# Image strips of eight rows in place of eight columns, and the last image stored in three parts

## The chip, the cores and the metric

The kernel runs on one core of one Trainium2 chip, with its five engines: PE (matmuls), DVE, ACT, POOL, and SP, which here only issues transfers. The metric is the device time of one execution in microseconds, the median of several runs.

## The reference, cut to what matters

The input is 32 images of 128 channels and 56 x 56 pixels in fp32; the output has the same shape. Each image passes through two residual blocks:

```python
x = x + _L0_conv_ref(_gn(x), ...)   # a gate for each channel, from the channel means
x = x + _L1_conv_ref(_gn(x), ...)   # dilated local attention

# in _L1_conv_ref, with KS = 3 and DILS = (1, 2, 4):
value = _conv1x1(x, v_w, v_b)
keyf  = _proj(x, k1_w, ..., k2_be, k2_m, k2_v)    # conv1x1, bn, relu, twice
query = _proj(x, q1_w, ..., q2_be, q2_m, q2_v)
uk = jnp.concatenate([_unfold3(keyf, d) for d in DILS], axis=2)    # 27 neighbours
uv = jnp.concatenate([_unfold3(value, d) for d in DILS], axis=2)
sim = jax.nn.softmax(jnp.sum(uk * query[:, :, None], axis=1, keepdims=True), axis=2)
return _conv1x1(jnp.sum(sim * uv, axis=2), w_w, w_b)
```

The 27 neighbours lie at steps of 1, 2 and 4 pixels, in rows and columns alike, so that the neighbourhood stays the same when rows and columns of the image change places. Group norm takes means over whole channels, in which the order of the pixels does not matter.

## The kernel before, in words

Channels lie on the 128 partitions. An image is one contiguous run of 3136 fp32 numbers in each partition of the tile `raw`, which has four such buffers (`RAWS`). The kernel cuts each image into seven strips of eight image columns (56 x 8 pixels, `SPIX` = 448), and each strip into seven units of 8 x 8 pixels. Attention runs over 25 tiles of two units. A tile takes a score matmul (`scores`, L473), a mask with a running minimum on DVE (`masked`, L1036), an exponential on ACT (L652), a scaling on DVE (`scaled`, L1050 and L1053), two transposes (L487), a copy on ACT (L667) and the matmuls with the values into `ps_o` (`context`, L508 and L513).

Five operations of a strip read or write `raw` in the order of a strip:

- `hidden` (L527) is the first projection on PE. It streams the whole strip as the moving operand; PE takes an fp32 matmul in two passes, so that one `hidden` stands in the trace as two matmuls. The second projection (L534) streams the contiguous tile `hid` of the same size.
- `shifted` (L870) on POOL scales and shifts the strip in place, once PE has read it.
- `spread` (L897) on POOL copies normalised blocks, offset by four columns against the strips, into `xb`, with three instructions for a block (six for the first, which is made of two half blocks). These are the stationary operands of the value matmuls (`values`, L553).
- `final` (L1061) on DVE adds the attention's result from PSUM to the strip in place. It counts up `o_done`.

The channel sums (L1092) read the image in flat pieces of 448 numbers, and loads and stores move it whole.

The order of work is written out by hand. All engines walk through the same sequence of images and slots, 25 slots for an image, and tables such as `G_SLOT`, `X1_SLOT`, `V_SLOT` and `BLOCK_SLOT` give the slot at which a strip's step is issued, relative to slot 0 of its image (a negative number is a slot of the image before). Beside it runs a chain of small steps for the statistics of the images to come, at the slots in `CH`: p1, p3, p4, p7 and p11 are POOL's steps, d1 to d13 DVE's, c1 to c6 PE's, a4 and a6 ACT's. The waits of POOL in L811 (p1), L830 (p4) and L843 (p7) belong to it, as does DVE's L1136 (d9), a copy out of the PSUM bank `ps_v`, which `values` writes next.

On SP, `keys` and `values` issue copies between partitions, `load` fetches an image three ahead, and `store` writes an image once all seven strips are final. The store of an image is issued at slot `STORE` = 13 of the next one; the last image's at slot `FINAL` = 6 of the drain, the slots after the last image.

In the two accessors of `raw` the strip is a pattern of 56 steps of 56 numbers with 8 adjacent numbers each:

```python
raw[:, m.offset % RAWS, :].rearrange("p (r c) -> p r c", c=W)[:, :, SIDE * s:SIDE * (s + 1)]
```

Of the kernel before, what the change touches and what calls it, by code (L numbers as in the profile page):

```python
# [13 lines left out]
NIMG = 32  # L14
ROUND = 4
ROUNDS = (NIMG - 4) // ROUND
H = W = 56
# [9 lines left out]
STRIPS = 7  # L27
SIDE = 8
UPIX = SIDE * SIDE
SPIX = UNITS * UPIX  # L30
# [10 lines left out]
RAWS = 4  # L41
# [4 lines left out]
SCALE, TRANSPOSE, CONTEXT, FINAL = 1, 3, 5, 6  # L46
# [19 lines left out]
LOAD = 19  # L66
STORE = 13
PIECES = 4

AWAKE = {CH["c3"]: 9, CH["c4"]: 5}  # L70

# [126 lines left out]
def build(nc, x, par, w1, w2, wv, wo, bo, bv, wg, out):  # L198
    with ExitStack() as ctx:
# [46 lines left out]
        raw = sb("raw", [P, RAWS, RAWPIX])  # L246
# [37 lines left out]
        def strip_of(m, s):  # L284

            return raw[:, m.offset % RAWS, :].rearrange(
                "p (r c) -> p r c", c=W)[:, :, SIDE * s:SIDE * (s + 1)]

        in_par, in_w = sem("in_par"), sem("in_w")
        g_const = sem("g_const")  # L290
# [2 lines left out]
        in_wg = sem("in_wg")  # L293
        x_piece = [sem(f"x_piece{i}") for i in range(PIECES - 1)]
        g_zs = sem("g_zs")
# [37 lines left out]
        o_done = event("o_done", STRIPS)  # L333
# [40 lines left out]
        def col(c, n=1):  # L374
            return g1[:, c:c + n]
# [5 lines left out]
        def images(first, last, drain=0, register=None):  # L381

            with nc.Block() as block:
                @block.sync
                def _(sp):
# [3 lines left out]
                    def load(m):  # L389
                        sp.wait_ge(stored[m.parity()].sem, stored[m.parity()].count(m + -4, 16))  # L390
                        sp.wait_ge(x_in[m.parity()].sem, x_in[m.parity()].count(m + -2, 16))
                        if m.offset == 0:
                            for i in range(PIECES):
                                pixels = slice(2 * BATCH * i, min(2 * BATCH * (i + 1), RAWPIX))
                                sp.dma_start(raw[:, 0, pixels], x[m.index(), :, pixels]).then_inc(
                                    x_piece[i] if i < PIECES - 1 else x_in[0].next(16), 16)
                            return
# [2 lines left out]
                        sp.dma_start(raw[:, m.offset % RAWS, :],  # L400
                                     x[m.index(), :, :]).then_inc(x_in[m.parity()].next(16), 16)

                    def store(m):
                        sp.wait_ge(o_done.sem, o_done.count(m, STRIPS))
                        sp.dma_start(out[m.index(), :, :],
                                     raw[:, m.offset % RAWS, :]
                                     ).then_inc(stored[m.parity()].next(16), 16)

                    def keys(m, g):
# [27 lines left out]
                    def slot(n, t):  # L437
                        if t == (LOAD if n.offset != -1 else 0) and (n + 3).exists():
                            load(n + 3)
                        for m, rel in items_at(n, t):  # L440
                            for g, at in enumerate(g_slots(m)):
                                if rel == at + 2:
                                    keys(m, g)
                            for s in (1, 3, 5):
                                if rel == V_SLOT[min(s + 2, COLUMNS - 1)] + 1:
                                    values(m, s)
                        if t == (STORE if n.exists() else FINAL) and (n + -1).exists():
                            store(n + -1)

                    for n, t in slots(first, last, drain, register):  # L450
                        slot(n, t)
# [287 lines left out]
                def _(gp):  # L739
                    n = [0]  # L740
# [132 lines left out]
                    def spread(m, b):  # L873
                        i, half = divmod(b, 2)
                        if b == 0:
                            gp.wait_ge(pg.sem, pg.count(m, 31))
                            gp.wait_ge(x_in[m.parity()].sem, x_in[m.parity()].count(m, 16))
                            if m.offset == 0:
                                for piece in x_piece:
                                    gp.wait_ge(piece, 16)  # L880
                        gp.wait_ge(v_ps.sem, v_ps.count(m + -1, min(2 * i + 2, COLUMNS)))
                        rows = raw[:, m.offset % RAWS, :].rearrange("p (r c) -> p r c", c=W)
                        if b == COLUMNS - 1:
                            to = xb[:, i, :, :, :].rearrange("p n h k -> p (n h) k")[:, 0:CHUNKS, :]
                        else:
                            to = xb[:, i, :, half, :]
                        to = to.rearrange("p n (r c) -> p n r c", c=SIDE)
                        if b == 0:
                            parts = ((slice(0, HALO), slice(W - HALO, W)), (slice(HALO, SIDE), slice(0, HALO)))
                        else:  # L890
                            parts = ((slice(0, SIDE), slice(SIDE * b - HALO, SIDE * b + HALO)),)
                        for cs, at in parts:
                            for k, rs, src in ((0, slice(0, HALO), rows[:, H - HALO:H, at]),
                                               (0, slice(HALO, SIDE), rows[:, 0:HALO, at]),
                                               (slice(1, CHUNKS), slice(0, SIDE), rows[:, HALO:H - HALO, at].rearrange(
                                                   "p (n r) c -> p n r c", r=SIDE))):
                                last = gp.tensor_scalar(to[:, k, rs, cs], src, col(Y_A + m.parity()),  # L897
                                                        col(Y_B + m.parity()), ALU.mult, ALU.add)
                        last.then_inc(xb_done.next(), 1)
# [309 lines left out]
```

## Time and profile before

| what | us |
|---|---|
| median of 3 runs | 1479.59 (1479.5 to 1479.63) |
| the profiled execution's own time | 1480.63 |
| its span, from the first to the last instruction | 1478.9 |
| PE busy | 1445.5 |
| DVE busy | 1256.4 |
| ACT busy | 1169.7 |
| POOL busy | 914.7 |

All times below come from the profiled execution. It took 1.04 us more than the median of the runs, and 1.73 us of its time lie outside its span. The mean granted clock of PE was 0.997 of full speed.

### The profile page before, as it was taken

What the parts mean: (1) busy time and instruction counts of PE and PEld (TensorE: products, weight loads), DVE (VectorE), ACT (ScalarE), POOL (GpSimd) and SP (SyncE); (2) the same over time, 40 slices, a digit from 0 to 9 for tenths busy, and PEclk for the clock granted to TensorE, in tenths of its full rate; (3) what the DMA queues carried; (4) which work ended last, traced back from release to release, by engine and by line L of the source; (5) the groups of instructions that cost most, each with busy time, mean ns of one, the idle gap of its engine ahead of it and who ended that gap; (6) DMA issues with size and microseconds to landing.
All of it is one profiled execution on the core that took longest, in us unless ns stands there. A gap on an engine that the chain in (4) does not pass through costs nothing.

```text
span 1478.9 us, 34970 instructions
## 1 busy us (share of the span) xinstructions
PE 1445.5 (98%) x9123; PEld 1180.4 (80%) x9123; DVE 1256.4 (85%) x4602; ACT 1169.7 (79%) x3047; POOL 914.7 (62%) x2049
## 2 busy tenths in 40 slices
PE   5899999999999999999999999999999999999998
PEld 2688888888888888888888888888888888888886
DVE  7788888888888888888888888888888888888876
ACT  3688888788878788778788778888878888787886
POOL 5766566576666575665675665665665765665730
PEclk9999999999999999999999999999999999999999
DMA  3334554445554345554345554445544455544344
GB/s 137 86 95 151 171 154 127 119 144 154 161 163 127 110 144 163 155 166 117 113 148 167 155 156 109 128 151 170 155 127 122 140 154 164 161 127 112 101 117 145
DMA packets 104706, 205.95 MB, mean 139 GB/s; under 512 B 13632, under 2 KB 83776, under 8 KB 96448
## 3 DMA queue, kind: packets, MB, share of 16 engines
q1 hardware_dynamic: 103632, 203.49, 46.4%
q8 instruction: 79, 1.29, 0.4%
q14 instruction: 115, 0.94, 0.2%
q10 hardware_dynamic: 880, 0.23, 0.1%
HBM read 51.62 MB, written 51.38 MB: 70 GB/s over the span
## 4 chain that ended last, share of the span: by engine, by line
PE 96%; issue 1%; POOL 1%; ACT 0%; DVE 0%; ACTq 0%; POOLq 0%; DVEq 0%
PE ps_s L473 24%; PE ps_o L508 20%; PE ps_v L553 12%; PE ps_t L487 12%; PE ps_p L527 11%; PE ps_p L534 11%; PE ps_o L513 3%; PE ps_v L573 0%; PE ps_v L576 0%; PE ps_v L569 0%; PE ps_v L580 0%; PE ps_t L534 0%; ACT qq L686 0%; POOL hats L831 0%; ACT hid L675 0%
## 5 line engine op out<-in xcount | busy, mean ns | idle before, releaser
L652 ACT ACTIVATE e<-e,zmin 128x256 f32<-128x256 f32 x800 | 403.1, 504 | 154.4 <-DVE zmin L1036 150.6
L1036 DVE CUSTOM_DVE_ANT_0 e<-ps_s,mask 128x256 f32<-128x256 f32 x800 | 337.3, 422 | 146.8 <-PE ps_s L473 138.6
L508 PEld LDWEIGHTS ps_o<-eT,v 128*128 128x128 f32 x2688 | 380.3, 191 | 82.9 <-issue 70.2
L508 PE MATMUL ps_o<-eT,v 128*128 128x128 f32 x2688 | 430.3, 275 | 0.4 <-ACT eT L667 0.3
L473 PE MATMUL ps_s<-kk,qq 128*128 128x256 f32 x1408 | 427.6, 386 | 1.7 <-DVE zmin L1036 1.7
L897 POOL TENSOR_SCALAR xb<-raw,g 128x32 f32<-128x32 f32 (+3 forms) x768 | 353.8, 476 | 0.0
L487 PE MATMUL ps_t<-ident,e 128*128 128x128 f32 x1600 | 305.7, 273 | 0.0
L487 PEld LDWEIGHTS ps_t<-ident,e 128*128 128x128 f32 x1600 | 225.2, 141 | 80.5 <-issue 0.2
L667 ACT ACTIVATE eT<-ps_t 128x512 f32<-128x512 f32 (+1 forms) x416 | 236.8, 569 | 63.9 <-PE ps_t L487 60.5
L1053 DVE SCALAR_TENSOR_TENSOR e<-e,rz,keep 128x256 f32<-128x256 f32 x480 | 254.6, 530 | 17.1
L473 PEld LDWEIGHTS ps_s<-kk,qq 128*128 128x128 f32 x1408 | 223.6, 192 | 49.0 <-issue 40.5
L553 PE MATMUL ps_v<-wvoT,xb 128*128 128x128 f32 x1580 | 214.7, 276 | 3.8 <-issue 0.2
L527 PE MATMUL ps_p<-raw,w1x 128*128 128x448 f32 x448 | 207.7, 545 | 1.1 <-ACT hid L675 0.7
L534 PE MATMUL ps_p<-hid,w2T 128*128 128x448 f32 x442 | 203.9, 543 | 1.8 <-ACT hid L675 1.8
L553 PEld LDWEIGHTS ps_v<-wvoT,xb 128*128 128x128 f32 x1580 | 193.8, 192 | 10.4 <-issue 10.4
L686 ACT ACTIVATE qq<-ps_p,bn_t 64x192 f32<-64x192 f32 x442 | 195.0, 441 | 7.6
L870 POOL TENSOR_SCALAR raw<-raw,g 128x448 f32<-128x448 f32 x224 | 175.8, 789 | 33.2 <-PE ps_p L527 33.2
L697 ACT ACTIVATE kk<-ps_p,bn_t 64x448 f32<-64x448 f32 x221 | 139.5, 631 | 36.0 <-PE ps_p L534 23.5
L652 ACT ACTIVATION_READ_ACCUMULATOR e<-e,zmin 128x1 f32 x800 | 150.9, 189 | 0.0
L675 ACT ACTIVATE hid<-ps_p,b1x 128x448 f32<-128x448 f32 x224 | 140.5, 627 | 12.3 <-PE ps_p L527 8.8
L1050 DVE TENSOR_SCALAR e<-e,rz 128x256 f32<-128x256 f32 x320 | 134.1, 419 | 11.4
L1061 DVE TENSOR_TENSOR raw<-raw,ps_o 128x448 f32<-128x448 f32 x224 | 137.6, 614 | 3.8 <-PE ps_o L513 1.7
(150 smaller groups left out, 1550.9 us busy)
## 6 DMA issues: line engine op xcount, KB each, us to landing
out_dram<-raw SPq DMA_DIRECT2D x32, 1568.0 KB, 5.7
raw<-in_x_dram SPq DMA_DIRECT2D x31, 1568.0 KB, 6.6
v<-v SPq DMA_DIRECT2D x192, 224.0 KB, 2.9
kk<-kk SPq DMA_DIRECT2D x192, 112.0 KB, 2.2
ksp<-kk SPq DMA_DIRECT2D x192, 64.0 KB, 2.1
v<-v_last SPq DMA_DIRECT2D x64, 128.0 KB, 2.9
kk<-kk SPq DMA_DIRECT2D x32, 224.0 KB, 2.9
v<-v_last SPq DMA_DIRECT2D x64, 96.0 KB, 2.7
```

The source lines that it names most:

```text
L473: nc.tensor.matmul(ps_s[i][:, 0:KEYS].rearrange("p (s h k) -> p h s k", s=2, h=2), qq[:, t, :], window.rearrange("p h (s k) -> p h s k", s=2),
L487: last = nc.tensor.transpose(o[:, base:base + KEYS].rearrange("p (a s k) -> p s a k", a=2, s=2)[:, i], e[:, t % RING, P * i:P * (i + 1)], ...
L508: last = nc.tensor.matmul(o[:, UPIX * (u - 1):UPIX * (u + 1)], v[:, s, u, :], eT[:, UPIX * (base + 2 * u - 1):UPIX * (base + 2 * u + 1)], ...
L527: nc.tensor.matmul(ps_p[:, 0:SPIX].rearrange("p (r c) -> p r c", c=SIDE), w1x[:, m.parity(), :], strip_of(m, g), start=True, stop=True).th ...
L534: nc.tensor.matmul(qk_bank(m, g)[:, 0:SPIX], w2T[:], hid[:], start=True, stop=True).then_inc(qk_ps.next(), 1)
L553: last = nc.tensor.matmul(v_bank(m, b)[:, P * j:P * (j + 1)], pixels, wvoT[:], start=True, stop=True)
L652: nc.scalar.activation(e[:, i, :], e[:, i, :], ACT.Exp, bias=zmin[:, i:i + 1], scale=-1.0, accum_out=zs[:, i:i + 1]).then_inc(e_done.next( ...
L667: nc.scalar.activation(eT[:, base:base + size], ps_t[(EPAIRS * n.parity() + j) % 2][:, 0:size], ACT.Copy).then_inc(eT_done.next(), 1)
L686: last = nc.scalar.activation(qq[HD * b:HD * (b + 1), at:at + len(units), UPIX * b:UPIX * (b + 1)], src[:, units[0]:UNITS:2, :], ACT.Relu, ...
L897: last = gp.tensor_scalar(to[:, k, rs, cs], src, col(Y_A + m.parity()), col(Y_B + m.parity()), ALU.mult, ALU.add)
L1036: nc.vector.tensor_tensor_reduce(e[:, i, :], ps_s[(TILES * n.parity() + t) % 2][:, 0:KEYS], mask[:].rearrange("p s h a b -> p (s h a b)"), ...
L1053: nc.vector.scalar_tensor_tensor(e[:, i, :], e[:, i, :], rz[:, i:i + 1], keep[:, KINDS.index(outside(t)), :], ALU.mult, ALU.mult).then_inc ...
```

## The change

The image in `raw` is read with rows and columns exchanged: the pattern "p (c r) -> p r c" with r = 56 takes the slow index of the memory as the column. A strip, still the slice of eight "columns", thereby holds eight image rows, which are 448 adjacent numbers in memory. The order inside an instruction stays the same for the other operands: 56 steps outside and 8 inside. So the eight inner numbers now lie 56 numbers (224 bytes) apart, and the outer step is one number. This holds for the reads of `hidden` and `spread`, and for the reads and writes of `shifted` and `final`. All other tiles (`xb`, `hid`, `kk`, `qq`, `v`, `e`) keep their layout, and the number and the sizes of the instructions on PE, DVE, ACT and POOL stay the same.

Since three adjacent strips are now one contiguous piece, `store` takes a range of strips. The last image is stored in three parts: strips 0 to 2 in slot 17 of the image, strips 3 to 5 in slot 24, and strip 6 in slot 6 of the drain. All other images are stored whole as before.

```diff
+LAST_STORES = {17: (0, 3), 24: (3, 6)}
...
         def strip_of(m, s):
 
             return raw[:, m.offset % RAWS, :].rearrange(
-                "p (r c) -> p r c", c=W)[:, :, SIDE * s:SIDE * (s + 1)]
+                "p (c r) -> p r c", r=H)[:, :, SIDE * s:SIDE * (s + 1)]
...
-                    def store(m):
-                        sp.wait_ge(o_done.sem, o_done.count(m, STRIPS))
-                        sp.dma_start(out[m.index(), :, :],
-                                     raw[:, m.offset % RAWS, :]
+                    def store(m, first=0, last=STRIPS):
+                        sp.wait_ge(o_done.sem, o_done.count(m, last))
+                        pixels = slice(SPIX * first, SPIX * last)
+                        sp.dma_start(out[m.index(), :, pixels],
+                                     raw[:, m.offset % RAWS, pixels]
                                      ).then_inc(stored[m.parity()].next(16), 16)
...
-                        if t == (STORE if n.exists() else FINAL) and (n + -1).exists():
+                        if t == STORE and n.exists() and (n + -1).exists():
                             store(n + -1)
+                        if n.offset == NIMG - 1 and t in LAST_STORES:
+                            store(n, *LAST_STORES[t])
+                        if n.offset == NIMG and t == FINAL:
+                            store(n + -1, STRIPS - 1, STRIPS)
...
-                        rows = raw[:, m.offset % RAWS, :].rearrange("p (r c) -> p r c", c=W)
+                        rows = raw[:, m.offset % RAWS, :].rearrange("p (c r) -> p r c", r=H)
```

## Rows read from the trace of the kernel before

**Rows 1.** The page: busy time of each engine; the chain that ended last.

```profile
PE 1445.5 (98%) x9123; PEld 1180.4 (80%) x9123; DVE 1256.4 (85%) x4602; ACT 1169.7 (79%) x3047; POOL 914.7 (62%) x2049
...
PE 96%; issue 1%; POOL 1%; ACT 0%; DVE 0%; ACTq 0%; POOLq 0%; DVEq 0%
```

**Rows 2.** Busy time of each engine over one image in the middle.

```profile
903.00:947.70 44.70, 44.60 (x284) 36.60 (x284) 38.71 (x143) 36.24 (x96) 28.42 (x64) 1.00 0.48 144
```

**Rows 3.** The end of the span in order of time: start, us, engine, line.

```profile
1470.23 0.61 DVE L1061 TENSOR_TENSOR raw<-raw,ps_o 128x448 f32<-128x448 f32 x1
...
1473.16 0.34 SPq L405 DMA_DIRECT2D out_dram<-raw  x1
```

**Rows 4.** The same for SP alone.

```profile
1457.98 15.51 SPq L405 DMA_DIRECT2D out_dram<-raw  x2
```

**Rows 5.** Waits of SP: us in total, times, longest.

```profile
SPq L405 <- DVE raw L1061: 14.6, 1, 14.6
SPq L454 <- DMA out_dram<-raw: 4.8, 1, 4.8
```

**Rows 6.** Transfers by issue: count, KB each, median us to landing.

```profile
v<-v SPq DMA_DIRECT2D x192, 224.0 KB, 2.9
...
par_s<-in_par_dram SPq DMA_DIRECT2D x1, 5.0 KB, 1.6
```

**Rows 7.** Groups by line and form on PE: busy us, mean ns of one.

```profile
L527 PE MATMUL ps_p<-raw,w1x 128*128 128x448 f32 x448 | 207.7, 545 | 1.1 <-ACT hid L675 0.7 <-POOL w1x L864 0.4
L534 PE MATMUL ps_p<-hid,w2T 128*128 128x448 f32 x442 | 203.9, 543 | 1.8 <-ACT hid L675 1.8
```

**Rows 8.** PE in order of time, around one `hidden` (two passes).

```profile
905.11 0.92 PE L527 MATMUL ps_p<-raw,w1x 128*128 128x448 f32 x2
905.86 0.38 PE L508 MATMUL ps_o<-eT,v 128*128 128x128 f32 x2
```

**Rows 9.** Groups by line and form on DVE.

```profile
L1092 DVE BATCH_NORM_STATS2 stats<-raw 128x6 f32<-128x448 f32 x224 | 138.0, 620 | 0.2
L1061 DVE TENSOR_TENSOR raw<-raw,ps_o 128x448 f32<-128x448 f32 x224 | 137.6, 614 | 3.8 <-PE ps_o L513 1.7
...
L940 DVE TENSOR_REDUCE spread_s<-ident 128x4 f32<-128x128 f32 x1 | 0.4, 378 | 0.0
...
L1008 DVE TENSOR_SCALAR bv_row<-ones,bv_s 128x128 f32<-128x128 f32 x1 | 0.3, 275 | 0.0
```

**Rows 10.** Groups by line and form on POOL.

```profile
L870 POOL TENSOR_SCALAR raw<-raw,g 128x448 f32<-128x448 f32 x224 | 175.8, 789 | 33.2 <-PE ps_p L527 33.2
...
L897 POOL TENSOR_SCALAR xb<-raw,g 128x384 f32<-128x384 f32 x192 | 139.8, 728 | 0.0
...
L897 POOL TENSOR_SCALAR xb<-raw,g 128x32 f32<-128x32 f32 x384 | 138.7, 371 | 0.0
...
L897 POOL TENSOR_SCALAR xb<-raw,g 128x16 f32<-128x16 f32 x128 | 44.3, 354 | 0.0
L897 POOL TENSOR_SCALAR xb<-raw,g 128x192 f32<-128x192 f32 x64 | 37.6, 588 | 0.0
```

**Rows 11.** Waits of POOL: us in total, times, longest.

```profile
POOL of_x L811 <- DVE of_x L1097: 208.2, 31, 7.0
...
POOL hats L830 <- ACT hats L723: 125.0, 31, 4.2
...
POOL of_x L843 <- DVE g L1133: 57.5, 30, 1.9
```

**Rows 12.** All engines in order of time, where PE waits in each image.

```profile
946.69 0.75 DVE L1053 SCALAR_TENSOR_TENSOR e<-e,rz,keep 128x256 f32<-128x256 f32 x1
...
947.26 0.38 PE L487 MATMUL ps_t<-ident,e 128*128 128x128 f32 x2
947.36 0.15 DVE L1136 COPY in_x<-ps_v 128x6 f32<-128x6 f32 x1
...
947.77 0.79 PE L553 MATMUL ps_v<-wvoT,xb 128*128 128x128 f32 x5
```

## The prediction

> **What bounds the kernel now.** I read the page first. The reader is to see that PE is busy for 98% of the span and makes up 96% of the chain that ended last [rows 1]: PE's stream sets the time, and whatever lengthens or stalls it is paid in full. The view by windows shows the same for one image in the middle, 44.70 us long: PE is idle for 0.10 us of it, DVE for 44.70 - 38.71 = 5.99, POOL for 44.70 - 28.42 = 16.28 [rows 2]. Then I read the end in order of time. The last strip becomes final, the last store is issued at 1473.16 and takes 0.34 us to issue [rows 3], and SP waits another 4.8 us for it to land [rows 5]: 5.1 us of nothing but a 1568 KB transfer. Last come the groups of the five operations that the edit touches [rows 7, 9, 10], and the order of time where PE does stall a little [rows 12].
>
> **The change, part by part.**
>
> *The store of the last image.* What ends the span is the transfer after the last `final`. It now carries one strip, 1568 / 7 = 224 KB. The trace has no 224 KB store, so I bound it. A 5 KB transfer lands in 1.6 us [rows 6]. If that is the fixed part, 1568 KB take 5.1 - 1.6 = 3.5 us more, a seventh of which is 0.5: 2.1 us. From the other side, a 224 KB copy inside the chip takes 2.9 us, among others [rows 6]. I take 2.4, nearer to the first, because at the end nothing else moves. The gain is 5.1 - 2.4 = 2.7 us (2.2 to 3.0).
>
> The two parts stored ahead cost nothing, and this is their cover. SP issues the store of the image before at 1457.98 [rows 4], and then sits for 14.6 us until the last strip is final [rows 5]; no copy of keys or values and no load is left behind it in its queue. Strips 0 to 2 fall into this wait. The store of strips 3 to 5 makes SP wait for strip 5, which is final at 1470.23 + 0.61 = 1470.84 [rows 3]. What is queued behind it is only the last part, ready at 1473.16, and an issue takes 0.34 us. Its 672 KB land, by the same two terms, 1.6 + 3.5 x 3/7 = 3.1 us after 1470.9, at about 1474.0; the last part would land at 1473.16 + 2.4 = 1475.6. Were the last part's bytes to move only after that, they would still end by 1474.0 + 0.5 = 1474.5 plus a completion, inside the bound of 2.9. Without the cover the two issues would cost below 1 us.
>
> *`hidden` on PE.* It is 224 matmuls of two passes [rows 7], read in steps of 224 bytes where eight adjacent numbers were read before. Two passes occupy 905.86 - 905.11 = 0.75 us [rows 8], 0.375 us for each, 0.84 ns a number. Runs of eight cost nothing against a contiguous operand: 545 ns beside 543 [rows 7]. No row of PE shows a run of one. The lower bound is 0: I see no reason for a gain, since the stream is already at the pace of the contiguous one. For the upper bound the nearest row is on another engine. DVE's L940 reads `ident` in steps of 4 numbers (16 bytes) and takes 378 ns for 128 numbers, where the elementwise L1008 takes 275 for 128 [rows 9]: at most 103 / 128 = 0.80 ns more a number, if all of it is the step and none the reduction. On PE that is 448 x 0.80 = 0.36 us a pass, 448 x 0.36 = 161 us in all, close to one doubling of the stream (448 x 0.375 = 168 us). Nothing covers this: PE is the bound. I take 0, because runs of eight are free on PE and L940 is another operation on another engine, but only just, and keep both ends.
>
> The Trainium skill speaks against the change here. "Advanced Engine Details and Errata", section SBUF Cachelines, says that SBUF is read in lines of 16 bytes, that at least two hits on a line are needed to hide the latency of the memory, and that a different line at each access costs something. It gives no price. By this rule every number of a strip is a line of its own, and the sum would be 1480 - 3 + 161 = 1638, not 1477; the rows with runs of eight don't test it, and L940 agrees with it without proving it.
>
> *`final` on DVE.* 224 instructions of 614 ns, with runs of eight as fast as L1092 on 448 contiguous numbers (620) [rows 9]. Bounds: 0, and by L940 448 x 0.80 = 0.36 us each, 7 x 0.36 = 2.5 us an image out of 5.99 idle. So DVE would stay below PE, but one place has no slack. In a stream without a stop the next matmul starts before the record of the last one ends, by 905.11 + 0.92 - 905.86 = 0.17 us [rows 8]. The transposes L487 end at 947.26 + 0.38 = 947.64, so that the value matmuls L553 could start at 947.47; they start at 947.77, 0.3 us late, after DVE's copy L1136 out of `ps_v` [rows 12]. A `final` stands in DVE's queue shortly before; if it takes 0.36 us more, L1136 comes late by that much and PE with it: 31 x 0.36 = 11 us. I take 0, as eightfold runs are free here too.
>
> *`shifted` and `spread` on POOL.* POOL is the one engine where runs show. From 32 to 384 numbers in runs of eight it takes 728 - 371 = 357 ns for 352 (1.01 ns each); from 16 to 192 in runs of four, 588 - 354 = 234 for 176 (1.33) [rows 10]. That is 8.1 ns for a run of eight and 5.3 for a run of four: 0.70 a number and 2.5 a run. Runs of one by this line would take 3.2 ns a number, 448 x 2.2 = 1.0 us more for a strip. The inner loop still has eight steps, so the lower bound is 0. Fourteen such strips an image (seven shifts, seven blocks) make 14 us at most, against 16.28 idle [rows 2]. POOL's waits are where it goes: 208.2 / 31 = 6.7 us before p1, 4.0 before p4, 1.9 before p7 [rows 11]. Between p3 and p4 the slot tables put four blocks and one shift; at 1.0 us each p4 would be 5.0 - 4.0 = 1.0 us late, DVE waits for it in its queue with the masks behind, and 31 images pay 31 us. Up to 0.8 us a strip this stays hidden. I take about 0.4, the middle of the lower half, because the loop keeps its length and only the step of the reads grows; it costs nothing on the path.
>
> The skill's "GPSIMD Engine Reference", section Performance pitfalls for Q7 kernels, gives about one cycle a number more for steps above 8 bytes, an estimated 0.37 us for 448 numbers; no row here shows it, and by it the sum stays as it is.
>
> *Sum*, against the profiled execution: 1480.63 - 2.7 + 0 = 1477.9, span 1476.2. This execution stood 1.04 us above the median of the runs; for the median I expect 1479.59 - 2.7 = 1476.9.
>
> **The rivals.**
>
> 1. *PE pays for far steps* (ends slower). Place: L527, all 448 passes. Price: 0.36 to 0.375 us a pass, 161 to 168 us; 1479.6 - 2.7 + 161 to 168 = 1638 to 1645. It decides early: 2.7 us / 448 = 6 ns a pass cancels the gain. For it: L940 and PE's lack of slack. Against it: runs of eight are free, and PE asks for a number only every 0.84 ns. This is also where the skill's line rule would lead.
> 2. *Only DVE or POOL pay.* `final` at 0.36 us more reaches PE through L1136: 1476.9 + 11 = 1488. L1136 also stands behind the L1053 of 0.75 us [rows 12]; both engines read SBUF there, and I can't exclude that longer POOL instructions stretch it. With POOL at its upper bound it is 1476.9 + 31 = 1508. Together they end at about 1519. It decides from 2.7 / 31 = 0.09 us a strip.
> 3. *The tail gains nothing*: the last part queues behind strips 3 to 5, or its landing is all fixed cost. Then 1479.6. The 1.6 us of the 5 KB transfer speak against it.
>
> **How the numbers follow.** Measurement here tells 0.2% (3.0 us) from no change. No price that reaches PE: 0.50, at 1476 to 1478, with 1476.9 the likeliest single value; since 2.7 lies just below 3.0, I split it 0.22 faster and 0.28 same (rival 3 is in the latter, with 0.05). Rival 2: 0.18, of which 0.03 same and 0.15 slower. Rival 1: 0.32, all slower. So faster 0.22, same 0.31, slower 0.47: the likeliest case is the small gain, though the two that lose weigh nearly as much together. A range that leaves out at most 2 in 10 has to reach rival 1: 1475.5 to 1648. The likeliest case alone has 1476 to 1478.
>
> **What would show it in the profile after.** Right: L527 still at 545 ns with 0.75 us to the next matmul, L1061 at 614, SP's last wait near 2.1 instead of 4.8, and an image of 44.7 us. L870 and L897 may grow without harm. Wrong: L527 near 900 ns and an image of about 50 us (rival 1); L527 unchanged, but L1061 or L870 longer, and a longer stop ahead of L553 or at POOL's hats (rival 2); SP's last wait still above 4 us (rival 3).

## The result and the profile after

The kernel after takes 1714.8 us (1713.37 to 1717.63), beside 1479.61 for the kernel before on the same chip: a ratio of 1.1586 [1.1572, 1.16], 235 us slower. The prediction of 1476.9, and its range up to 1648, were wrong. The profiled execution took 1715.77 us with a span of 1714.0 at a granted clock of 0.996, so the clock is not the reason. Line numbers are six higher after than before (`hidden` is L533, `final` L1067, `shifted` L876, `spread` L903), but two higher for `store` (L407).

The page of the kernel after, busy time and the chain that ended last:

```profile
PE 1661.9 (97%) x9123; PEld 1192.6 (70%) x9123; DVE 1423.2 (83%) x4602; ACT 1189.6 (69%) x3047; POOL 1111.6 (65%) x2049
...
PE 89%; DVE 5%; issue 3%; POOL 1%; ACT 1%; DVEq 0%; ACTq 0%; POOLq 0%
```

The counts of instructions are those of [rows 1]. PE is busy for 1661.9 - 1445.5 = 216 us more, and its idle time grows from 33 to 52 us; DVE and POOL are busy for 167 and 197 us more. In the chain PE's share falls from 96% to 89% and DVE's rises to 5%: PE is still the bound, and is now also kept waiting.

The groups by line and form in the kernel after (busy us, mean ns of one, idle time before):

```profile
L533 PE MATMUL ps_p<-raw,w1x 128*128 128x448 f32 x448 | 406.1, 997 | 6.6 <-issue 5.4 <-ACT hid L681 0.7 <-POOL w1x L870 0.4
...
L1059 DVE SCALAR_TENSOR_TENSOR e<-e,rz,keep 128x256 f32<-128x256 f32 x480 | 312.2, 650 | 17.1
...
L876 POOL TENSOR_SCALAR raw<-raw,g 128x448 f32<-128x448 f32 x224 | 277.5, 1247 | 35.1 <-PE ps_p L533 35.1
...
L1067 DVE TENSOR_TENSOR raw<-raw,ps_o 128x448 f32<-128x448 f32 x224 | 222.1, 992 | 3.3 <-PE ps_o L519 1.2
...
L903 POOL TENSOR_SCALAR xb<-raw,g 128x384 f32<-128x384 f32 x192 | 203.6, 1060 | 0.0
L540 PE MATMUL ps_p<-hid,w2T 128*128 128x448 f32 x442 | 203.0, 541 | 2.3 <-ACT hid L681 2.3
...
L1056 DVE TENSOR_SCALAR e<-e,rz 128x256 f32<-128x256 f32 x320 | 169.0, 528 | 11.4
```

All four operations of the edit have grown against [rows 7, 9, 10]: `hidden` from 545 to 997 ns, `final` from 614 to 992, `shifted` from 789 to 1247, the large block of `spread` from 728 to 1060. The neighbour L540, whose operand is contiguous, kept its time (543 and 541). L1059 and L1056 are not part of the edit: they are the two forms of the scaling, which were L1053 and L1050 in the kernel before, and their means have grown from 530 to 650 ns and from 419 to 528:

```profile
L1053 DVE SCALAR_TENSOR_TENSOR e<-e,rz,keep 128x256 f32<-128x256 f32 x480 | 254.6, 530 | 17.1
...
L1050 DVE TENSOR_SCALAR e<-e,rz 128x256 f32<-128x256 f32 x320 | 134.1, 419 | 11.4
```

PE in order of time, one `hidden` of two passes and its successor:

```profile
908.49 1.80 PE L533 MATMUL ps_p<-raw,w1x 128*128 128x448 f32 x2
910.11 0.63 PE L514 MATMUL ps_o<-eT,v 128*128 128x128 f32 x4
```

Two passes occupy 910.11 - 908.49 = 1.62 us, against 0.75 in [rows 8]: 1.81 ns a number in place of 0.84, 0.87 us more for each of 224 `hidden`.

All engines in order of time, at the place in each image where [rows 12] showed PE 0.3 us late:

```profile
943.10 2.35 POOL L876 TENSOR_SCALAR raw<-raw,g 128x448 f32<-128x448 f32 x2
...
944.29 1.43 DVE L1059 SCALAR_TENSOR_TENSOR e<-e,rz,keep 128x256 f32<-128x256 f32 x1
...
945.64 0.15 DVE L1142 COPY in_x<-ps_v 128x6 f32<-128x6 f32 x1
...
946.04 1.13 PE L559 MATMUL ps_v<-wvoT,xb 128*128 128x128 f32 x8 [0.80 <-DVE squares L1143]
```

L1059 takes 1.43 us here and 0.48 at other times (at 942.59, for one). It starts while POOL runs two `shifted`, from 943.10 to 945.45, and ends 0.27 us after them. The copy L1142 out of `ps_v` stands behind it, and PE's value matmuls L559 stop for 0.80 us.

Taken instruction by instruction, the trace shows that this is no single case. Of the 480 L1059, 151 last longer than 0.6 us, and every one of them ends 0.25 to 0.28 us after the end of a POOL instruction that ran beside it; 100 of the 320 L1056 last longer than 0.47 us and end 0.14 to 0.16 us after one.

SP's last wait (us in total, times, longest), and the last `final`:

```profile
SPq L460 <- DMA out_dram<-raw: 1.6, 1, 1.6
```

```profile
1710.51 0.97 DVE L1067 TENSOR_TENSOR raw<-raw,ps_o 128x448 f32<-128x448 f32 x1 [1.16 <-PE ps_o L519]
```

The tail did what was forecast: SP's last wait is 1.6 us, not 4.8 [rows 5]. The span ends 1714.0 - 1711.48 = 2.5 us after the last `final` ends.

### The profile page after: what moved, and what is told of

The parts are those of the page before. It is cut to its first block, busy times and chain, and to the rows that moved or that the text cites. A ratio compares the mean times of both kernels' runs of the same rounds, so it can differ in the third digit from the quotient of the medians.

```text
span 1714.0 us, 34972 instructions
## 1 busy us (share of the span) xinstructions
PE 1661.9 (97%) x9123; PEld 1192.6 (70%) x9123; DVE 1423.2 (83%) x4602; ACT 1189.6 (69%) x3047; POOL 1111.6 (65%) x2049
## 4 chain that ended last, share of the span: by engine, by line
PE 89%; DVE 5%; issue 3%; POOL 1%; ACT 1%; DVEq 0%; ACTq 0%; POOLq 0%
PE ps_p L533 22%; PE ps_s L479 19%; PE ps_o L514 16%; PE ps_p L540 10%; PE ps_v L559 10%; PE ps_t L493 9%; PE ps_o L519 3%; DVE e L1059 2%; DVE e L1042 1%; DVE v L1080 1%; PE ps_v L579 0%; ACT e L658 0%; PE ps_t L540 0%; PE ps_v L575 0%; PE ps_v L586 0%
## 5 line engine op out<-in xcount | busy, mean ns | idle before, releaser
L514 PEld LDWEIGHTS ps_o<-eT,v 128*128 128x128 f32 x2688 | 390.2, 195 | 268.6 <-issue 210.4
L903 POOL TENSOR_SCALAR xb<-raw,g 128x32 f32<-128x32 f32 (+3 forms) x768 | 453.5, 604 | 0.0
L514 PE MATMUL ps_o<-eT,v 128*128 128x128 f32 x2688 | 435.6, 277 | 0.4 <-ACT eT L673 0.4
L533 PE MATMUL ps_p<-raw,w1x 128*128 128x448 f32 x448 | 406.1, 997 | 6.6 <-issue 5.4
L1059 DVE SCALAR_TENSOR_TENSOR e<-e,rz,keep 128x256 f32<-128x256 f32 x480 | 312.2, 650 | 17.1
L876 POOL TENSOR_SCALAR raw<-raw,g 128x448 f32<-128x448 f32 x224 | 277.5, 1247 | 35.1 <-PE ps_p L533 35.1
L559 PE MATMUL ps_v<-wvoT,xb 128*128 128x128 f32 x1580 | 219.9, 280 | 21.1 <-DVE squares L1143 19.1
L1067 DVE TENSOR_TENSOR raw<-raw,ps_o 128x448 f32<-128x448 f32 x224 | 222.1, 992 | 3.3 <-PE ps_o L519 1.2
L559 PEld LDWEIGHTS ps_v<-wvoT,xb 128*128 128x128 f32 x1580 | 194.3, 192 | 34.8 <-issue 24.5
L540 PE MATMUL ps_p<-hid,w2T 128*128 128x448 f32 x442 | 203.0, 541 | 2.3 <-ACT hid L681 2.3
L1056 DVE TENSOR_SCALAR e<-e,rz 128x256 f32<-128x256 f32 x320 | 169.0, 528 | 11.4
L817 POOL TENSOR_SCALAR of_x<-spread_s,of_x 128x4 f32<-128x4 f32 x32 | 9.7, 304 | 258.8 <-DVE of_x L1103 258.8
```

What stands on the lines that cost most here:

```text
L514: last = nc.tensor.matmul(o[:, UPIX * (u - 1):UPIX * (u + 1)], v[:, s, u, :], eT[:, UPIX * (base + 2 * u - 1):UPIX * (base + 2 * u + 1)], ...
L533: nc.tensor.matmul(ps_p[:, 0:SPIX].rearrange("p (r c) -> p r c", c=SIDE), w1x[:, m.parity(), :], strip_of(m, g), start=True, stop=True).th ...
L540: nc.tensor.matmul(qk_bank(m, g)[:, 0:SPIX], w2T[:], hid[:], start=True, stop=True).then_inc(qk_ps.next(), 1)
L559: last = nc.tensor.matmul(v_bank(m, b)[:, P * j:P * (j + 1)], pixels, wvoT[:], start=True, stop=True)
L876: gp.tensor_scalar(to, to, col(X_A + m.offset % RAWS), col(X_B + m.parity()), ALU.mult, ALU.add).then_inc(x1_done.next(), 1)
L1059: nc.vector.scalar_tensor_tensor(e[:, i, :], e[:, i, :], rz[:, i:i + 1], keep[:, KINDS.index(outside(t)), :], ALU.mult, ALU.mult).then_inc ...
```

## The experiments

The theory after the result: each engine pays when it takes only one number of a 16-byte line of `raw` before it goes to another (the rule on lines that the prediction quotes), whatever the distance; PE's part is paid in full, DVE's and POOL's reach PE through DVE's queue. The rivals: PE's 997 ns are contention with the longer DVE and POOL work; or the distance of the step counts, not the single hit; or DVE's and POOL's growth is hidden, as predicted. Steps of several sizes were tried on PE alone.

In all but the last two kernels the order of the pixels in a strip differs between operations, or from the order that attention assumes, so that their outputs are others; number and size of the instructions stay. Ratios are to the kernel before on the same chip; differences between two of the kernels below are differences of their ratios, times 1480 us. Kernels with an added accessor `flat_of` (a strip as 448 adjacent numbers) have lines ten higher than before (kernel 3, behind `hidden`, thirty).

**1. Nothing far.** The kernel after, with all four operations (`hidden`, `shifted`, `spread`, `final`) in the order of the memory; row strips and the three-part store stay.

```diff
+        def flat_of(m, s):
+
+            return raw[:, m.offset % RAWS, SPIX * s:SPIX * (s + 1)]
...
-                        nc.tensor.matmul(ps_p[:, 0:SPIX].rearrange("p (r c) -> p r c", c=SIDE), w1x[:, m.parity(), :],
-                                         strip_of(m, g), start=True, stop=True).then_inc(h_ps.next(), 1)
+                        nc.tensor.matmul(ps_p[:, 0:SPIX], w1x[:, m.parity(), :],
+                                         flat_of(m, g), start=True, stop=True).then_inc(h_ps.next(), 1)
...
-                        to = strip_of(m, s)
+                        to = flat_of(m, s)
...
-                        to = to.rearrange("p n (r c) -> p n r c", c=SIDE)
+                        to = to.rearrange("p n (c r) -> p n c r", r=SIDE)
...
-                                                   "p (n r) c -> p n r c", r=SIDE))):
-                                last = gp.tensor_scalar(to[:, k, rs, cs], src, col(Y_A + m.parity()),
+                                                   "p (n r) c -> p n c r", r=SIDE))):
+                                last = gp.tensor_scalar(to[:, k, cs, rs], src, col(Y_A + m.parity()),
...
-                        to = strip_of(n, s)
+                        to = flat_of(n, s)
...
```

> The strips stay eight image rows and the last image is stored in three parts, but all operations on them read and write their numbers in the order of memory (runs of 448, in the spread runs of eight), so that the pixels of a strip stand in another order than the attention assumes. This leaves the tail alone. In the profile after, the span ends 2.5 us after the last final (5.8 before), so theory and rivals alike expect 1479.6 - 3.2 = 1476.4 us, 45 us an image inside, no instruction longer than before. If the three stores cost something of their own, it shows here: above 1477.

Measured: 1477.5 us, ratio 0.9975 [0.9967, 0.9984], 3.7 us faster than before (2.4 to 4.9). SP's waits in it:

```profile
SPq L464 <- DMA out_dram<-raw: 1.6, 1, 1.6
```

The bound of 1477 in the expectation was set against 1479.6; on this chip the kernel before took 1480.9, so that the ratio decides, and the three stores show no cost of their own. So the whole slowdown comes from the order of access, and the store in parts is worth about 3.7 us. This kernel is the base of the next ones.

**2. Only `hidden` far.** Kernel 1, with PE reading as in the kernel after.

```diff
-                        nc.tensor.matmul(ps_p[:, 0:SPIX], w1x[:, m.parity(), :],
-                                         flat_of(m, g), start=True, stop=True).then_inc(h_ps.next(), 1)
+                        nc.tensor.matmul(ps_p[:, 0:SPIX].rearrange("p (r c) -> p r c", c=SIDE), w1x[:, m.parity(), :],
+                                         strip_of(m, g), start=True, stop=True).then_inc(h_ps.next(), 1)
```

> As the run without far steps, but the first projection alone reads in far steps (pixel order of the other operations as there). Theory (each number that lies in another place costs PE 0.97 ns by itself): two passes take 1.62 us, 224 x 0.87 = 195 us, so 1476.4 + 195 = 1671. Rival, contention (PE is slow because DVE and POOL read in far steps too): the two passes take clearly less than 1.62 us and the time stays below 1640. Rival, cover (DVE and POOL cost nothing, and all 238 us are PE's): 1710 or more.

Measured: 1665.68 us, ratio 1.1246 [1.123, 1.1261], 188 us above kernel 1. The group by line and form:

```profile
L537 PE MATMUL ps_p<-raw,w1x 128*128 128x448 f32 x448 | 405.6, 996 | 1.1 <-ACT hid L685 0.7 <-POOL w1x L874 0.4
```

996 ns with DVE and POOL at their old pace, 997 after: contention falls, the price is PE's own. The rival by which it is all of the slowdown (1710 or more) falls too. The stream grows by 224 x 0.87 = 195 us, and the page has PE busy for 1641.9 us against 1446.6 in kernel 1, also 195. But PE's idle time shrinks from 29.7 to 23.1 us, which makes the 188. What went is the stop before the value matmuls that [rows 12] show: measured from the start of one matmul to the start of the next, beyond what the same two lines take without a stop, it is 30 times 0.27 us in kernel 1, 8.0 us in all, and none here.

**3. Which step pays on PE.** Kernel 1, where `hidden` takes each of the seven strips of an image in another order.

```diff
+                        pixels = flat_of(m, g)
+                        if g == 0:
+                            done = nc.tensor.matmul(ps_p[:, 0:SPIX], w1x[:, m.parity(), :], pixels, start=True, stop=True)
+                        if g == 1:
+                            done = nc.tensor.matmul(ps_p[:, 0:SPIX].rearrange("p (b a) -> p b a", b=2), w1x[:, m.parity(), :],
+                                                    pixels.rearrange("p (a b) -> p b a", b=2), start=True, stop=True)
...
+                        if g == 5:
+                            done = nc.tensor.matmul(ps_p[:, 0:SPIX].rearrange("p (b a c) -> p b a c", b=28, c=2), w1x[:, m.parity(), :],
+                                                    pixels.rearrange("p (a b c) -> p b a c", b=28, c=2), start=True, stop=True)
...
```

> As the run without far steps, but the first projection reads each of the seven strips with another pattern (its pixels are then in another order): strip 0 contiguous, strips 1 to 4 in steps of 2, 4, 8 and 64 numbers, strips 5 and 6 in runs of 2 and of 4 numbers that lie 56 apart. Theory of lines of 16 bytes: steps of 4, 8 and 64 all cost what a step of 56 costs (record near 1.0 us a pass), step 2 and runs of 2 are free or cost half as much, runs of 4 are free (0.54 us). Rival, distance (the far jump or a clash of banks at 224 bytes makes the cost): step 4 and 8 are cheap, 56 and 64 differ, and runs of 2 or 4 still pay for each jump.

Measured: 1547.88 us, a single execution; the comparison is between strips of the same execution. The groups by line and form; the lines are, in order: steps of 8 numbers, of 4, of 64, contiguous, runs of two 56 apart, steps of 2, runs of four 56 apart.

```profile
L547 PE MATMUL ps_p<-raw,w1x 128*128 128x448 f32 x64 | 56.6, 975 | 0.0
L544 PE MATMUL ps_p<-raw,w1x 128*128 128x448 f32 x64 | 55.6, 958 | 0.0
L550 PE MATMUL ps_p<-raw,w1x 128*128 128x448 f32 x64 | 53.7, 928 | 0.0
L539 PE MATMUL ps_p<-raw,w1x 128*128 128x448 f32 x64 | 31.6, 575 | 0.4 <-POOL w1x L894 0.4
L553 PE MATMUL ps_p<-raw,w1x 128*128 128x448 f32 x64 | 31.5, 573 | 0.0
L541 PE MATMUL ps_p<-raw,w1x 128*128 128x448 f32 x64 | 30.6, 559 | 0.7 <-ACT hid L705 0.7
L556 PE MATMUL ps_p<-raw,w1x 128*128 128x448 f32 x64 | 29.4, 540 | 0.0
```

There are two levels and nothing between. Steps of 4 numbers (16 bytes) pay the full price, and 8 or 64 no more; steps of 2, and runs of two that lie 56 numbers apart, pay nothing. The distance falls as a rival; what counts is whether two numbers in a row come from one 16-byte piece of memory. No strip took a step of 3 or a run of two across the border of such a piece, so that the fixed borders of a line matter, and not only a step below 16 bytes, is not shown here.

**4. Only `final` far.** Kernel 1, with DVE as in the kernel after.

```diff
-                        to = flat_of(n, s)
+                        to = strip_of(n, s)
                         nc.vector.tensor_tensor(
-                            to, to, ps_o[(STRIPS * n.parity() + s) % 2][:, 0:SPIX],
+                            to, to, ps_o[(STRIPS * n.parity() + s) % 2][:, 0:SPIX].rearrange("p (r c) -> p r c", c=SIDE),
```

> As the run without far steps, but DVE's final alone reads and writes in far steps (the pixel order is wrong as there). Theory (final reaches PE only where DVE's copy out of ps_v is late): 0.38 us once an image, 1477.5 + 12 = 1490. Rival, DVE is the engine that makes the 97 us of the run with PE in memory order: 1550 or more. Rival, it hides: 1478.

Measured: 1492.08 us, ratio 1.0079 [1.0065, 1.0093]; by the ratios 15 us above kernel 1 (13 to 18). PE's waits:

```profile
PE ps_v L563 <- DVE in_x L1146: 6.7, 28, 0.3
PE ps_p L537 <- issue: 6.4, 30, 0.2
```

`final` takes 996 ns with POOL at its old pace: its price, too, is its own. The first row is the place that the prediction named: the copy (here L1146) comes late out of DVE's queue, once an image, and the value matmuls (L563) wait. Most of this stop was there before, though: from start to start of the matmuls it is 11.8 us, and 8.0 in kernel 1, so that this way costs 3.8 us. The second row is the larger part. From start to start, `hidden` stops 31 times for 0.39 us, 11.5 us in all, and not once in kernel 1. The row names no releaser beyond "issue", but the order of time shows one:

```profile
928.54 0.99 DVE L1071 TENSOR_TENSOR raw<-raw,ps_o 128x448 f32<-128x448 f32 x1
...
929.45 0.41 DVE L1046 CUSTOM_DVE_ANT_0 e<-ps_s,mask 128x256 f32<-128x256 f32 x1
...
929.90 0.51 ACT L662 ACTIVATE e<-e,zmin 128x256 f32<-128x256 f32 x1 [0.88 <-DVE zmin L1046]
...
930.52 0.90 ACT L696 ACTIVATE qq<-ps_p,bn_t 64x256 f32<-64x256 f32 x2
...
931.52 0.99 PE L537 MATMUL ps_p<-raw,w1x 128*128 128x448 f32 x2 [0.23 <-issue]
```

The mask of a tile (L1046) stands behind `final` in DVE's queue, ACT's exponential (L662) waits for the mask, the queries (L696) stand behind the exponential in ACT's queue, and the next `hidden` waits for the queries in its code: it starts 0.10 us after they end. The two ways make 3.8 + 11.5 = 15.3 of the 15 us.

**5. Only `shifted` and `spread` far.** Kernel 1, with POOL as in the kernel after.

```diff
-                        to = flat_of(m, s)
+                        to = strip_of(m, s)
...
-                        to = to.rearrange("p n (c r) -> p n c r", r=SIDE)
+                        to = to.rearrange("p n (r c) -> p n r c", c=SIDE)
...
```

> As the run without far steps, but POOL's shift and spread alone use far steps (pixel order wrong as there). Theory (longer POOL instructions stop DVE, whose instructions with two inputs in SBUF wait for POOL's to end; that makes DVE late and PE with it): most of the 97 us, 1477.5 + 60 to 85 = 1538 to 1563, with single instructions of DVE of about 1 us. Rival of the prediction (POOL's extra time lies in its own waits and costs nothing): 1478 to 1480.

Measured: 1562.69 us, ratio 1.0557 [1.0543, 1.0571], 86 us above kernel 1. The groups by line and form on DVE and POOL:

```profile
L1063 DVE SCALAR_TENSOR_TENSOR e<-e,rz,keep 128x256 f32<-128x256 f32 x480 | 296.7, 618 | 17.2
L880 POOL TENSOR_SCALAR raw<-raw,g 128x448 f32<-128x448 f32 x224 | 289.2, 1300 | 23.4 <-PE ps_p L537 23.4
...
L1102 DVE BATCH_NORM_STATS2 stats<-raw 128x6 f32<-128x448 f32 x224 | 137.6, 618 | 0.2
...
L1119 DVE SCALAR_TENSOR_TENSOR cells<-pooled_row,conv 128x128 f32<-128x128 f32 x96 | 48.1, 546 | 1.1
...
L1111 DVE SCALAR_TENSOR_TENSOR squares<-in_x 128x4 f32<-128x4 f32 x32 | 29.1, 910 | 1.1
```

The same DVE lines in kernel 1:

```profile
L1063 DVE SCALAR_TENSOR_TENSOR e<-e,rz,keep 128x256 f32<-128x256 f32 x480 | 253.2, 527 | 17.1
...
L1119 DVE SCALAR_TENSOR_TENSOR cells<-pooled_row,conv 128x128 f32<-128x128 f32 x96 | 23.0, 288 | 1.1
...
L1111 DVE SCALAR_TENSOR_TENSOR squares<-in_x 128x4 f32<-128x4 f32 x32 | 5.2, 163 | 1.1
```

None of the DVE lines was edited. Yet L1063 grew from 527 ns to 618, L1119 from 288 to 546, and L1111, which works on four numbers, from 163 to 910; L1102, which streams 448 numbers of `raw`, stayed at 620 and 618. So it is no general slowing: certain DVE instructions stop while a POOL instruction runs. Of the 480 L1063, 94 last longer than 0.6 us; in each case a POOL instruction had begun before, nearly always a `shifted`, and L1063 ends 0.25 to 0.28 us after that instruction's end. L1111 stops beside `shifted`, too, L1119 beside `spread`. They stand ahead of what PE waits for:

```profile
PE ps_v L563 <- DVE in_x L1146: 28.1, 29, 1.0
PE ps_o L518 <- ACT eT L677: 19.1, 30, 0.7
PE ps_p L544 <- ACT hid L685: 15.4, 60, 1.3
```

These waits make 63 us; another 24.5 us stand in PE's busy time (1471.1 against 1446.6), since the ends of its records are modelled. From start to start of the matmuls, the stops at these three places are 34.0, 24.4 and 23.9 us, and 8.0, 0.9 and 0.4 in kernel 1: 73 us more, of the 86.

**6. All far but `hidden`.** The kernel after, with PE in the order of the memory.

```diff
-                        nc.tensor.matmul(ps_p[:, 0:SPIX].rearrange("p (r c) -> p r c", c=SIDE), w1x[:, m.parity(), :],
-                                         strip_of(m, g), start=True, stop=True).then_inc(h_ps.next(), 1)
+                        nc.tensor.matmul(ps_p[:, 0:SPIX], w1x[:, m.parity(), :],
+                                         flat_of(m, g), start=True, stop=True).then_inc(h_ps.next(), 1)
```

> The changed kernel with the first projection alone read in the order of memory (its pixels are then in another order); DVE's final and POOL's shift and spread keep their far steps. Theory: what PE did not pay itself remains, 1714.8 - 195 = 1520. Rival, cover: 1477, because DVE (992 ns a final) and POOL (1247 ns a shift) then still fit beside PE. If PE's slow passes had covered part of the others' cost in the changed kernel, it comes out above 1520.

Measured: 1574.38 us, ratio 1.0629 [1.0613, 1.0645], 97 us above kernel 1. Theory and rival were both wrong in size: DVE and POOL cost more than the bounds of the prediction, and far more than the rival's none. By the parts, 15 + 86 = 101 us: they nearly add. DVE and POOL in order of time:

```profile
1377.09 3.93 POOL L907 TENSOR_SCALAR xb<-raw,g 128x32 f32<-128x32 f32 x6
...
1378.13 1.06 DVE L1119 SCALAR_TENSOR_TENSOR cells<-pooled_row,conv 128x128 f32<-128x128 f32 x1
...
1379.38 0.32 DVE L1119 SCALAR_TENSOR_TENSOR cells<-pooled_row,conv 128x128 f32<-128x128 f32 x1
...
1380.03 1.01 DVE L1123 TENSOR_SCALAR g<-g 128x3 f32<-128x3 f32 x1
```

Within one stretch of POOL's `spread`, the same L1119 takes 1.06 us and then 0.32; L1123, on three numbers, takes 1.01 us against a mean of 185 ns in kernel 1. That is a stop until a POOL instruction has ended, not a slower stream: all 31 L1119 over 0.6 us end 0.14 to 0.15 us after the end of a `spread` instruction, and all 30 L1123 over 0.3 us end 0.02 to 0.03 us after one.

**7. `hidden` and `final` far, POOL not.** Kernel 2 with the edit of kernel 4.

```diff
-                        to = flat_of(n, s)
+                        to = strip_of(n, s)
...
```

> The changed kernel with shift and spread on POOL in memory order (shift exact, the order inside the spread's blocks changed); PE's first projection and DVE's final keep their far steps. Theory (POOL's share of the 49 us that the changed kernel has above the run with PE alone far is the larger one): 1666 to 1685. Rival, DVE's share is the larger one: 1695 to 1715.

Measured: 1678.53 us, ratio 1.1333 [1.1316, 1.135]; 13 us above kernel 2, of which stops before `hidden` make 11.7 from start to start, 0.10 us behind the queries as in kernel 4; before the value matmuls there is no stop. The scaling on DVE, by line and form:

```profile
L1063 DVE SCALAR_TENSOR_TENSOR e<-e,rz,keep 128x256 f32<-128x256 f32 x480 | 243.3, 507 | 17.1
```

From here to the kernel after is POOL alone: 1.1586 - 1.1333 = 0.0253, 37 us, and the scaling goes from 507 to 650 ns. The four steps lead from the kernel before to the kernel after one by one, so that their sum, -3.7 + 188 + 13 + 37 = 234 of 235, holds by construction; the size of a step depends on its place, as POOL's 86 us alone and 37 here show.

**8. Contiguous strips in runs of eight.** Row strips and the three-part store, but the eight inner numbers of a strip run down the memory: units are turned, and so are the mask, the border tables and the blocks of `xb`. The price is on ACT, which writes a strip's keys with four instructions in place of one.

```diff
-            return raw[:, m.offset % RAWS, :].rearrange(
-                "p (c r) -> p r c", r=H)[:, :, SIDE * s:SIDE * (s + 1)]
+            return raw[:, m.offset % RAWS, SPIX * s:SPIX * (s + 1)].rearrange(
+                "p (c u r) -> p u c r", c=SIDE, r=SIDE)
...
+                        src = qk_bank(m, g)[HD:P, 0:SPIX].rearrange("p (u h c j r) -> p h j u c r", h=2, c=HALO, j=2, r=HALO)
+                        for h in range(2):
+                            for j in range(2):
...
+                                last = nc.scalar.activation(to, src[:, h, j], ACT.Relu, bias=bn_t[HD:P, 1:2])
...
```

> A version of the changed kernel that computes the reference: strips are eight image rows and the last image is stored in three parts, but inside each unit of 8 x 8 pixels the order is turned, so that every operation on the image has runs of eight again. The mask, the border tables and the blocks turn with it; the write of the keys becomes four instructions of 112 numbers on ACT in place of one of 448. Theory of lines: PE, DVE and POOL as before the change, ACT some 0.6 us more a strip, 4 us of its 8.5 idle us an image: 1477.5 if that hides, as the run without far steps. Rival, ACT becomes late at the exponentials: 1485 to 1520.

Measured: 1491.85 us, ratio 1.0085 [1.0071, 1.0099], so the rival holds. The group by line and form on ACT:

```profile
L706 ACT ACTIVATE kk<-ps_p,bn_t 64x112 f32<-64x112 f32 x884 | 237.1, 343 | 43.1 <-PE ps_p L540 30.3
```

Four instructions take 4 x 343 = 1372 ns for a strip, where one of 448 took 631 before. That this is what ends up on the path is argued from ACT's growth, not shown by a wait.

**9. The same with two instructions for the keys.** The keys lie unit by unit over all columns, so that two instructions write a strip's and the score matmuls read them in order.

```diff
+        def keys_of(parts):
+
+            return kk[parts, :, :].rearrange("p a b -> p (a b)").rearrange("p (u c r) -> p u c r", u=PROWS // SIDE, r=SIDE)
...
+                        for j in range(2):
+                            rows = slice(HALO, SIDE) if j == 0 else slice(0, HALO)
+                            last = nc.scalar.activation(
+                                keys_of(slice(0, HD))[:, j:j + UNITS, SIDE * g + HALO:SIDE * (g + 1) + HALO, rows],
+                                src[:, j], ACT.Relu, bias=bn_t[HD:P, 1:2])
...
```

> The version with turned units, with the keys laid out unit by unit over all columns, so that ACT writes a strip's keys with two instructions of 224 numbers in place of four of 112 (343 ns each there, 631 for one of 448 before: 247 fixed and 0.86 a number, so two of 439). ACT is then 1.7 us an image above before instead of 5.2. It computes the reference. SP's copies of the keys take 7 pieces of 256 bytes a partition in place of one of 1792. Theory (the 14 us of the version with four writes are ACT's lateness): 1478 to 1481 against 1480 before, at best the 1477.5 of the run without far steps. Rival (the copies of many small pieces come late to the scores): 1490 or more, with PE's scores waiting for the copies of kk.

Measured: 1480.32 us, ratio 0.9991 [0.9982, 1.0]: equal to the kernel before within the measurement. The groups by line and form:

```profile
L536 PE MATMUL ps_p<-raw,w1x 128*128 128x448 f32 x448 | 207.6, 545 | 0.7 <-ACT hid L684 0.7
...
L706 ACT ACTIVATE kk<-ps_p,bn_t 64x224 f32<-64x224 f32 x442 | 172.4, 439 | 38.4 <-PE ps_p L543 25.8
...
L1073 DVE TENSOR_TENSOR raw<-raw,ps_o 128x448 f32<-128x448 f32 x224 | 137.7, 615 | 3.8 <-PE ps_o L522 1.7
```

With strips contiguous as in the kernel after, but runs of eight, the operations are back at their old times: 545 ns for `hidden` and 615 for `final`. What is left of the three-part store's 3.7 us is 1.3. The keys take 2 x 439 = 878 ns a strip in place of 631, which may be what eats the rest; no run separates it. Kernels 8 and 9 are the two in which all operations agree on the order of the pixels; 8 is slower than the kernel before, and 9 equal to it.

## Why the prediction was wrong

*What bounds the kernel*: right. PE's stream sets the time, and 188 of the 235 us are its own longer matmuls.

*`hidden` on PE: the step that failed.* "I take 0, because runs of eight are free on PE and L940 is another operation on another engine, but only just, and keep both ends." Runs of eight say nothing of runs of one: kernel 3 shows the price to be all or nothing, with everything from two numbers of a 16-byte line upward free. L940, a reduction on DVE, was the better witness, since its step was 16 bytes. The upper bound was too small as well: 0.36 us a pass by L940, 0.375 by one doubling; it measured (1.62 - 0.75) / 2 = 0.435, 195 us in all and not 161 to 168. That is why even rival 1 (1638 to 1645) fell short of kernel 2's 1665.68.

The rule of the Trainium skill that the prediction weighed and set aside ("Advanced Engine Details and Errata", section SBUF Cachelines) was right, and the runs agree with it: two hits on a 16-byte line are free (559 and 573 ns), one hit pays (958). The price that it does not give is 1.81 - 0.84 = 0.97 ns a number on PE in this kernel.

*`final` on DVE*: taken as 0, measured 378 ns (614 to 992), a little above the bound of 0.36 us. The way to PE that the prediction names (a copy out of `ps_v`, then the value matmuls) is there, but it carries 3.8 of the 15 us that `final` costs alone, and nothing beside the slow PE. The other 11.5 us, and 11.7 of the 13 beside the slow PE, came by a way that the prediction does not have: mask, exponential, queries, `hidden`. That its 11 us came near the 15 is luck.

*`shifted` and `spread` on POOL*: the size was about right, the consequence was not. `shifted` grew by 1247 - 789 = 458 ns where 0.4 us were taken, and the bound of 1.0 us held. "It costs nothing on the path" failed, because the prediction counted POOL's own slack and its hats. POOL had the time; it is the DVE instructions stopped by POOL's that come late. The trace of the kernel before had these stops already: 92 of its 480 L1053 last longer than 0.6 us (the others 0.49 at the median), and each ends 0.26 to 0.28 us after a POOL instruction. The L1053 of 0.75 us in [rows 12] is one of them; with a longer `shifted`, the same stop is longer. Rival 2 had the place ("I can't exclude that longer POOL instructions stretch it") but no price for it: at most 31 us were given, 86 came alone and 37 beside the slow PE. From start to start, the kernel after stops for 30.1 us before the value matmuls, where kernel 7 has no stop, and for at most 1.1 us each at the other two places that kernel 5 shows (24.4 and 23.9 us there). That a `hidden` of 1.62 us gives DVE the time to catch up there is argued, not shown.

The Trainium skill says this in "SBUF — State Buffer", section Who interferes with whom: a DVE instruction with two operands in SBUF shares a read path with a GpSimd instruction that reads SBUF, and one that finds it taken is blocked, while DVE instructions with one such operand are not, outside their two-port modes. The traces agree: L1059, L1119 and L1111 have two SBUF operands and stop, the one-operand L1102 does not (618 ns). The scaling L1056 has one tensor in SBUF and stops as well (419 to 528 ns); after POOL's end it needs 0.14 to 0.16 us for its 256 numbers, where L1059 needs 0.25 to 0.28. That pace, and the stop of L1123, fit the exception for two-port modes, but no view names the mode. The rule of the Trainium skill's "GPSIMD Engine Reference", section Performance pitfalls for Q7 kernels (about one cycle a number more for steps above 8 bytes), led the prediction to an estimate of 0.37 us for 448 numbers; 0.46 was measured.

*The rivals together.* 1 and 2 both came true. They were given chances apart and no case for both, which is one reason why the range ended below the result; the prices are the other, since even the upper bounds together make 1645 + 11 + 31 = 1687. The parts also overlap: DVE and POOL cost 97 us beside a fast PE, 50 beside the slow one.

*The tail*: right, a little larger. 2.7 us were forecast (2.2 to 3.0), 3.7 measured (2.4 to 4.9); SP's last wait is 1.6 where 2.1 were expected, and the 224 KB landed in 1.9 us, not 2.4:

```profile
out_dram<-raw SPq DMA_DIRECT2D x2, 672.0 KB, 3.4
...
out_dram<-raw SPq DMA_DIRECT2D x1, 224.0 KB, 1.9
```

The 672 KB were forecast at 3.1 and took 3.4, and the last part did not queue behind them.

## What to carry to other kernels

Before an access pattern is turned, count how many numbers in a row come from one 16-byte line: on PE two fp32 numbers were enough here (on DVE and POOL nothing between single numbers and eight was tried), and single ones cost about 1 ns a number on each of the three engines. In a trace with longer runs little shows that price beforehand; here it was one small reduction (L940). A longer POOL instruction is not hidden because POOL is idle: look for the DVE instructions that end a fixed time after a POOL instruction, here those with two operands in SBUF and the scaling with one, and for what stands behind them in DVE's queue. When two bad cases share a cause, give them a chance together.

## What the runs showed of the hardware that was not expected

- PE's price for single hits is a step, not a slope: 540 to 575 ns up to steps of 2 or from runs of two, 928 to 975 for steps of 4, 8 and 64 alike.
- It does not depend on what else runs: 996 ns alone, 997 with DVE and POOL slowed as well. The same holds for `final` on DVE: 996 ns alone, 992 beside slow PE and POOL.
- The price per number is nearly the same on three engines: 0.97 ns on PE (1.81 - 0.84), 378 / 448 = 0.84 on DVE, where the instruction reads and writes the strip, and 458 / 448 = 1.02 on POOL for `shifted`, 332 / 384 = 0.86 for the large block of `spread`.
- A DVE instruction on four numbers (L1111) took 910 ns on average, 163 without POOL's far reads: the stop lasts until the POOL instruction ends, and is not in proportion to the instruction's own work. Behind that end, L1063 needs another 0.25 to 0.28 us for 256 numbers, the scaling L1060 (L1056 in the kernel after) 0.14 to 0.16, L1123 0.02 to 0.03 for three.
